# The order of statistics, roots, gathers and gate sums around the two expert stages of a macaron block

## The reference

```
x = x + 0.5 * moe(layernorm(x))        # "layer 0" below
x = x + attention(layernorm(x))        # causal, one head of 256
x = x + 0.5 * moe(layernorm(x))        # "layer 1" below
```

## Time and profile before

| | us |
|---|---|
| median of 3 runs | 2091.16 |
| lowest, highest | 2090.38, 2092.34 |
| the profiled execution | 2092.78 |
| its span | 2091.0 |
| TensorE busy | 1912.9 (91%) |
| VectorE busy | 1483.1 (71%) |
| ScalarE busy | 1421.1 (68%) |
| GpSimd busy | 1244.8 (60%) |
| mean granted TensorE clock | 0.956 |

### The profile page before, as it was taken

The page is one execution under the profiler, slowest core; times in us unless marked ns, Lnnn a source line. Parts: engine busy times, 40 slices in busy tenths (PEclk is TensorE's granted clock), DMA queues, the critical chain, the costliest instruction groups (busy, mean ns, idle before and its releaser), DMA issues. The chain is left out here.

```text
span 2091.0 us, 41021 instructions
## 1 busy us (share of the span) xinstructions
PE 1912.9 (91%) x14588; PEld 1328.4 (64%) x14588; DVE 1483.1 (71%) x4395; ACT 1421.1 (68%) x2740; POOL 1244.8 (60%) x1353
## 2 busy tenths in 40 slices
PE   8628999999999999899999999249999999999997
PEld 6514566666666666577777777126666666666665
DVE  8789767777777765389889998887656555555542
ACT  8755566767667676578888787656576676666664
POOL 5214787777777776644444442025877676767675
PEclk9759999999999999999999999669999999999999
DMA  8933456465556454545555554223555554645443
GB/s 276 337 114 76 118 93 124 87 109 109 99 97 102 93 87 64 116 123 159 160 158 146 149 148 109 93 70 95 105 106 100 114 102 94 122 94 98 77 75 38
DMA packets 361740, 242.25 MB, mean 116 GB/s; under 512 B 228928, under 2 KB 348992, under 8 KB 361280
## 3 DMA queue, kind: packets, MB, share of 16 engines
q1 hardware_dynamic: 304192, 172.34, 31.1%
q0 software_dynamic: 57344, 67.29, 21.4%
HBM read 121.03 MB, written 84.93 MB: 98 GB/s over the span
## 5 line engine op out<-in xcount | busy, mean ns | idle before, releaser
L1261 DVE SCALAR_TENSOR_TENSOR hid_l<-hf,hid_h 128x512 f16<-128x512 f32 x512 | 352.5, 700 | 339.6 <-ACT hid_h L702 335.1
L1482 PE MATMUL ps<-w_h,hid_h 128*128 128x256 f16 x2048 | 559.2, 273 | 0.0
L1483 PE MATMUL ps<-w_l,hid_h 128*128 128x256 f16 x2048 | 559.1, 273 | 0.0
L1484 PE MATMUL ps<-w_h,hid_l 128*128 128x256 f16 x2048 | 558.9, 273 | 0.0
L1482 PE MATMUL ps<-xt,w_h 128*128 128x512 f16 x1024 | 389.8, 381 | 19.8 <-ACT hf L806 16.6
L806 ACT ACTIVATE hf<-ps,b 128x512 f32<-128x512 f32 x512 | 345.4, 675 | 75.6 <-PE ps L1484 69.1
L1484 PE MATMUL ps<-xt,w_l 128*128 128x512 f16 x1024 | 390.1, 381 | 0.0
L1483 PE MATMUL ps<-xt,w_h 128*128 128x512 f16 x1024 | 389.9, 381 | 0.0
L702 ACT ACTIVATE ys<-yb,weight 128x256 f32<-128x256 f32 x256 | 128.0, 506 | 343.3 <-DVE yb L1279 337.1
L702 ACT ACTIVATE hid_h<-hf 128x512 f16<-128x512 f32 x512 | 322.4, 630 | 16.3
L589 POOL DMA_INDIRECT weight<-gate_d,gate_at x256 | 257.6, 1006 | 83.9 <-issue 76.5
(11 more groups left out here) (297 smaller groups left out, 3852.0 us busy)
## 6 DMA issues: line engine op xcount, KB each, us to landing
w_st<-fc_t SPq DMA_DIRECT2D x32, 1024.0 KB, 5.8
xin<-x SPq DMA_DIRECT2D x32, 512.0 KB, 5.1
xa<-x_d SPq DMA_DIRECT2D x32, 512.0 KB, 4.5
out<-x SPq DMA_DIRECT2D x32, 512.0 KB, 5.2
z_d<-z SPq DMA_DIRECT2D x32, 512.0 KB, 6.0
xt<-xs SPq DMA_TRANSPOSE x256
weight<-gate_d,gate_at POOLq DMA_INDIRECT x256
b_st<-fc_b SPq DMA_DIRECT2D x16, 128.0 KB
```

The costliest lines, as they stand in the source:

```text
L1261: dve.scalar_tensor_tensor(hid_l[:, n % 2, f, :], hf[:, f % HF, :], HS, hid_h[:, n % 2, f, :], ALU.mult, ALU.subtract).then_inc(s_hl, 1)
L1482: pe.matmul(dst, lh, rh, start=first, stop=False)
L1483: pe.matmul(dst, lh, rl, start=False, stop=False)
L1484: return pe.matmul(dst, ll, rh, start=False, stop=last)
```

## The change

On SP the copy of x waits until the scan is over (s_top), and w2_in of expert 1 moves ahead of the wait for the gates and their store. On POOL the root of chunk 1 goes ahead of gather(2), and gather(3) and root(3) ahead of gate_sums; at m = 3 and 4 the early scatter and the root of chunk m + 2 go ahead of weights(m). On VectorE the statistics of chunk 1 move up behind the third slot count, its shift up ahead of choice_2; the statistics at t == 3 go ahead of first_turns(m, 3), so that those of chunk 3 stand ahead of choice_8, the tiles and gate_scale. first_stats(2) moves from behind the third to behind the fourth quarter of the last fc2.

```
@@ SP
                 if layer == 0:
+                    sp.wait_ge(s_top, 1)
                     sp.dma_start(x1_d..., xf...).then_inc(s_copy, 16)
...
                 columns(N0 + 2)
+                w2_in(E0 + 1)
                 sp.wait_ge(s_gate, layer + 1)
                 sp.dma_start(gate_d..., gate[:, :, :]).then_inc(s_gate_d, 16)
-                w2_in(E0 + 1)
@@ POOL
                 gather(N0 + 1, TG // 2, TG)
+                roots(N0 + 1)
                 gather(N0 + 2)
-                roots(N0 + 1)
                 roots(N0 + 2)
+                gather(N0 + 3)
+                roots(N0 + 3)
                 gate_sums(layer)
-                gather(N0 + 3)
                 gates(layer)
-                roots(N0 + 3)
                 pool.wait_ge(s_gate_d, 16 * (layer + 1))
...
                     if m + 2 < LAST:
                         gather(N0 + m + 2)
+                    early = scattered(m)[:1] if m in (3, 4) else []
+                    if early:
+                        scatter(N0 + early[0])
+                        roots(N0 + m + 2)
                     if m < LAST:
                         weights(N0 + m)
-                    early = scattered(m)[:1] if m in (3, 4) else []
-                    for n in early:
-                        scatter(N0 + n)
-                    if m + 2 < LAST:
+                    if not early and m + 2 < LAST:
                         roots(N0 + m + 2)
@@ VectorE
                 count_slots(0, E0, 2)
+                rows_stats(N0 + 1)
                 if layer == 0:
                     router_halves()
                     attention_weights()
+                rows_shift(N0 + 1)
                 choice_2(layer)
                 for h in range(4):
                     w2_lo(E0, h)
-                rows_stats(N0 + 1)
...
                         if t == 0 and m + 1 < LAST:
-                            rows_shift(n + 1)
+                            if m > 0:
+                                rows_shift(n + 1)
                             rows_lo(n + 1)
+                        if t == 3 and m + 2 < LAST:
+                            rows_stats(n + 2)
                         if m < NC:
                             first_turns(m, t)
-                        if t == 3 and m + 2 < LAST:
-                            rows_stats(n + 2)
...
-                        if layer == 0 and (m, t) == (LAST, 2):
+                        if layer == 0 and (m, t) == (LAST, 3):
                             first_stats(2)
```

## The result

The changed kernel takes 2096.91 us (median of 16 runs, 2094.63 to 2101.30) against 2092.40 for the kernel before on the same chips (16 runs). The ratio is 1.0024, 95% interval [1.0017, 1.0031]: about 5 us slower. The forecast was 3.6 us faster. The profiled execution took 2098.05 us with a span of 2096.3; the one before took 2092.78 with 2091.0.

The account below looks back on a forecast made before the run. TensorE is 91% busy, so time comes only from its idle places, where VectorE was taken as the early-chunk bound. Sum +0.6 - 1.5 + 0.3 - 3.0 = -3.6 us, giving 2087.6 on the median; range 2082 to 2095.5.

Parts of the forecast that it names:

- (c): Layer 0, rest of GpSimd's queue about 7.2 us late; chunk 4's rows late, TensorE feels 0.75; balance +5.25.
- (b): Layer 0, gather(3), stats(3), root(3) ahead of gate_sums: VectorE stands at gate_scale, TensorE late at expert 1's pick; running balance +4.5.
- (a): Layer 0, chunk 1's statistics and shift earlier: one 6.0 us TensorE wait; net +0.5, bounds -1.0 and +0.8.
- (d): Layer 0, early scatter and root ahead of the weights, chunks 5 and 6: TensorE's gap at chunk 5 closes, -4.65.
- w2 loads: Layer 1: ScalarE's 7.62 us w2 wait and TensorE's 4.57 us gap go; layer balance -3.0, bounds -0.2 and -5.
- (f): Copy of x waits for the scan's end, ending at 146.3, first gather at 146.19: cost 0.3, bounds -0.5 and 4.
- (e): Attention start, first_stats(2) behind the last output bias: gain 1.5, bounds 0 and 4.
- a sign that it is wrong: VectorE not standing at gate_scale (forecast idle about 4.4 us in layer 0, 2.4 in layer 1).
- slow rival: Gate sums on GpSimd keep 7.5 us and the gap at chunk 5 stays: +5.9, 2097.1; chance 0.18.

Follow-up runs that it names:

- sums last: Kernel before with only the fourth chunk's gather, statistics and root ahead of the adds of the gate sums: 2102.71 us, ratio 1.0054.
- swap: Kernel before with only the early scatter and root ahead of the gate weights at chunks 3 and 4, both layers: 2090.77 us, ratio 0.9996.
- w2: Kernel before with only the loads of the second expert's w2 ahead of the wait for the gates: 2091.03 us, ratio 1.0000.
- VectorE moves: Kernel before with only the second chunk's statistics and shift (and root) earlier and first_stats(2) one step later: 2090.33 us, ratio 0.9999.
- copy: Kernel before with only the wait that starts the copy of the rows behind the scan: 2088.03 us, ratio 0.9983.
- split gates: Changed kernel with sums first, plus gates scaled and written in two parts, the first expert's ahead: 2082.20 us, ratio 0.9966 to the kernel before.
- sums first: Changed kernel with the fourth chunk's gather, statistics and root back behind the gate-sum adds: 2085.49 us, ratio 0.9970 to the kernel before.

## Why the prediction was wrong, step by step

**(c), the step that failed.** The prediction has GpSimd's queue late by about 7.2 us and says "of this TensorE feels 0.75". The lateness was forecast rightly (7.3 us in layer 0 of the changed kernel), its price was not. I looked for the next gap that a late root makes, and took the rest for absorbed. But the queue has no idle time up to chunk 4's weights: ScalarE waits 7.31 and 9.29 us for them, TensorE 2.45 and 5.13. In chunk 5 layer 0 goes from 2.6 us behind to 7.0 and layer 1 from 3.0 ahead to 4.3 behind, 11.7 us in all with what the clock takes, one or two chunks after the place where I stopped looking. The sum had nothing there. Up to there the sum for layer 1 was right: -3.0 forecast, -3.0 measured at the second pick.

**(b), right in its balance by luck, and stopped too early.** With (a) it was sized at +4.5 in layer 0 at the second pick, and +4.8 is measured there. But the way there is another: 5.7 us at the first pick, some 2.5 more by the clock, then the 4.29 us gap of before and its lower clock saved, then a wait of 2.40 us at the second pick. That wait lowers the clock again, and the third pick waits 1.62 us: +8.2, where (c) has +5.25. This edit alone measures +11.3 us in the whole. The sum has no term for TensorE's wait at the first pick (6.98 us). In the kernel before TensorE doesn't wait there, so a timeline kept to idle times doesn't show this meeting point, though the text has the tiles on VectorE behind the moved statistics.

**(d), early scatter and root: -4.65 forecast, -0.8 [-2.7, +1.0] measured alone.** The gap did close, and in layer 0 the weights of chunk 3 were in time. The weights of chunk 4, which the step moves just as far, were not looked at; they landed 7.3 us after ScalarE asked.

**Layer 1, w2 loads: -3.0 forecast (the layer's whole balance), 0.0 [-1.9, +1.9] measured alone.** Same failure as (c): the gap at chunk 2 went and came back at chunk 5, as the queue didn't start earlier.

**(f), the copy: +0.3 forecast, -3.6 [-5.4, -1.7] measured.** The sum only asked whether the copy is over in time (it is: issued at 86.8, 54.1 us long, landed at 140.9, the first gather behind it), and never what it does to the work beside it where it ran before. The bound of -0.5 had no row behind it.

**(a) and (e): -1.0 forecast, -0.2 [-2.1, +1.7] measured**, within what a measurement tells apart. TensorE's single wait ahead of chunk 1 came out at 5.47 us (6 forecast), and the balance behind it at +0.2 (+0.5 forecast).

**(b), in detail.** Right: VectorE stands for the rows of gather(3) (3.58 us, 2 forecast). Right in size by luck: TensorE's gap (6.98 us for 6 to 7, at another place and for another reason), and the sums, which take 5.1 us where 7.5 were measured before (5.5 forecast), with a last add of 0.51; they were to be short because VectorE stands, and it was at work. Wrong: VectorE hardly waits at gate_scale (0.35 us instead of 4.4; in layer 1 not at all instead of 2.4), which the prediction itself names as a sign that it is wrong. The two engines run beside each other there and VectorE's own tile operations are the slow ones, after and then before:
```profile
207.68 2.31 DVE L1196 TENSOR_SCALAR tile_of<-slot_row,first 128x512 f16<-128x512 f16 x1
209.91 1.42 DVE L1197 TENSOR_SCALAR below<-slot_row,last_of 128x512 f16<-128x512 f16 x1
211.36 0.90 DVE L1198 TENSOR_TENSOR tile_of<-tile_of,below 128x512 f16<-128x512 f16 x1
212.60 0.23 DVE L1185 TENSOR_SCALAR ginv<-gsum 128x128 f32<-128x128 f32 x1 [0.35 <-POOL gsum L562]
```
```profile
207.04 0.35 DVE L1194 TENSOR_SCALAR tile_of<-slot_row,first 128x512 f16<-128x512 f16 x1
207.31 0.35 DVE L1195 TENSOR_SCALAR below<-slot_row,last_of 128x512 f16<-128x512 f16 x1
207.69 0.42 DVE L1196 TENSOR_TENSOR tile_of<-tile_of,below 128x512 f16<-128x512 f16 x1
```
Before, GpSimd was gathering rows beside these three, after, it does the sums (207.43 to 212.57). In layer 1 of the changed kernel they take 1.25, 0.88 and 0.63, beside the sums as well. Moving the sums didn't remove the clash between VectorE and GpSimd, it moved it: the sums win 2.4 us, the tiles lose 3.5, and TensorE waits for the tiles.

The terms as measured alone: +11.3 (sums last) - 0.8 (swap) + 0.0 (w2) - 0.2 (VectorE moves) - 3.6 (copy) = +6.7 us; the whole change measures +5.0 [3.6, 6.5]. The single effects have intervals of about 2 us each, so the difference says nothing on how they combine. The account by layers is of single traces; the attention alone differs by up to 3.8 us among the fourteen. The slow rival had the right size (+5.9) for the wrong reason: the sums did not keep their 7.5 us and the gap at chunk 5's root did not stay.

What stays open: why TensorE stops for 3 us in the scan while the copy runs (the profile names no releaser), whether the version with split gates is faster than the one with the sums first, and how much of layer 0's loss is the queue's: there the wait at the first pick and the late queue always came together.

## What to carry to other kernels

When an edit makes a queue late, find the stretch in which that queue has no idle time and price the lateness at its end, not at the next wait behind the edit. A gap that closes upstream of such a queue is lent and given back, unless the queue starts earlier. A wait that an edit creates isn't among the idle times of the kernel before: follow each result that the edit delays to every engine that reads it. Before sizing a moved transfer by its landing, look at what ran beside it in its old place.

## What the runs showed of the hardware that I had not expected

- With a 16 MB copy from HBM to HBM beside the router's scan TensorE stops for 2.8 to 3.4 us with no releaser in the profile (seven profiles with it, none of seven without).
- 3.5 us of added GpSimd work cost 5.9 us of time: with the 4.48 us gap that it made, the granted clock is 0.92 over the 45 us around it. In the other kernels with a gap at chunk 5 of layer 1 it is 0.92 (gaps of 4.72 to 5.13 us), 0.96 (4.58 and 4.75) and 1.00 (2.38).
- Gaps of some 2.4 us go either way: behind 2.40 us the fc1 matmul takes 0.61 us at 289.56 of the swap alone, and the changed kernel's pick 0.59 us at 228.25; behind 2.45 us at 294.90 of the changed kernel and behind 2.38 us in the split gates it takes 0.39 us.
- The last add of the sums (128 by 128) takes 2.05 us in the kernel before, in both layers, where VectorE's scan of 896 columns runs beside it and the add ends 0.25 us behind the scan; it takes 0.45 and 0.51 us in the changed kernel, where VectorE works on the tiles. What ran beside this small GpSimd operation mattered more than its size: the first one, of 1024 columns, took 2.35 us. No run varied this alone.
